# Layer norm, routing and shared branch merged into one block, with the router's logits between the transposes, in a two-layer cross-attention and mixture-of-experts kernel

## The reference

```python
x = x + tanh(g_ffn[0]) * ffn0(layernorm(x))
...
x = x + tanh(g_ffn[1]) * ffn1(layernorm(x))

def ffn0(x, w1s, w2s, w3s, W1, W2, W3, Wg):        # 8 experts, width 1024, one per token
    shared = gelu(x @ w1s) * (x @ w2s) @ w3s
    idx = argmax(x @ Wg)
    return shared + geglu of expert idx
def ffn1(x, W_gate_router, expert_bias, Wg, Wu, Wd, Wg_s, Wu_s, Wd_s):   # 8 experts, width 192, two per token
    scores = sigmoid(x @ W_gate_router)
    sel = top_2(scores + expert_bias)
    w = scores[sel] / sum(scores[sel])
    return silu(x @ Wg_s) * (x @ Wu_s) @ Wd_s + sum_k w[k] * expert_sel[k](x)
```

## Time and profile before

| | us |
|---|---|
| median of 3 timed runs (1776.4 to 1784.43) | 1779.78 |
| the profiled execution's own time | 1767.28 |
| its span | 1765.5 |
| PE busy | 1484.7 (84%) |
| DVE busy | 1160.5 (66%) |
| ACT busy | 856.5 (49%) |
| POOL busy | 237.3 (13%) |

### The profile page before, as it was taken

The page is one execution under the profiler, slowest core; times in us unless marked ns, Lnnn a source line. Parts: engine busy times, 40 slices in busy tenths (PEclk is TensorE's granted clock), DMA queues, the critical chain, the costliest instruction groups (busy, mean ns, idle before and its releaser), DMA issues. The chain is left out here.

```text
span 1765.5 us, 23798 instructions
## 1 busy us (share of the span) xinstructions
PE 1484.7 (84%) x7833; PEld 870.6 (49%) x7834; DVE 1160.5 (66%) x2277; ACT 856.5 (49%) x1537; POOL 237.3 (13%) x357
## 2 busy tenths in 40 slices
PE   5769889779996999994499999999999999675883
PEld 3333333367885788883253333433443434553551
DVE  5739889464112677775399999999999973531334
ACT  3214777522212555551317777777777786231110
POOL 2000000001202333331000000000000000064443
PEclk9787999878998999997659999999999999697997
DMA  8844121120103899982533211111121100525114
GB/s 287 349 143 136 44 56 46 42 92 13 38 1 129 292 341 341 332 314 81 153 87 89 46 25 42 30 24 24 32 40 24 24 2 1 119 78 164 39 42 164
DMA packets 107534, 190.84 MB, mean 108 GB/s; under 512 B 10702, under 2 KB 80323, under 8 KB 107431
## 3 DMA queue, kind: packets, MB, share of 16 engines
q1 hardware_dynamic: 97521, 159.31, 28.7%
q0 software_dynamic: 7584, 27.93, 4.3%
q10 hardware_dynamic: 2326, 2.31, 0.4%
HBM read 145.20 MB, written 43.79 MB: 107 GB/s over the span
## 5 line engine op out<-in xcount | busy, mean ns | idle before, releaser
L1099 DVE TENSOR_REDUCE attend_piece_max<-attend_p_bank 128x1 f32<-128x400 f32 (+3 forms) x1280 | 669.5, 589 | 66.5 <-PE attend_p_bank L982 54.3
L1079 ACT ACTIVATE attend_probs<-attend_s_bank 128x512 f32<-128x512 f32 (+1 forms) x1053 | 549.6, 606 | 232.4 <-PE attend_s_bank L996 232.1
L982 PE MATMUL attend_p_bank<-attend_k_st,attend_q_st 62*128 62x400 f32 (+2 forms) x1280 | 416.0, 435 | 41.6 <-DMA attend_q_st<-q_rows 19.4
L996 PE MATMUL attend_s_bank<-attend_q_st,attend_k_st 64*128 64x512 f32 (+1 forms) x1053 | 390.3, 447 | 39.4 <-ACT attend_probs L1079 13.2
L996 PEld LDWEIGHTS attend_s_bank<-attend_q_st,attend_k_st 64*128 64x128 f32 (+1 forms) x1053 | 168.3, 184 | 347.3 <-ACT attend_probs L1079 326.0
L1013 PE MATMUL attend_o_bank<-attend_probs,attend_v_st 128*32 128x512 f32 (+1 forms) x2176 | 291.0, 607 | 2.2 <-ACT attend_probs L1079 2.1
L982 PEld LDWEIGHTS attend_p_bank<-attend_k_st,attend_q_st 62*128 62x128 f32 x1280 | 208.6, 195 | 89.4 <-issue 39.1
L1753 DVE TENSOR_TENSOR slots_w_low<-slots_w_up,slots_w_high 128x2048 fp32r<-128x2048 f32 x46 | 110.4, 2402 | 45.7 <-ACT slots_w_high L1749 45.7
L1540 DVE TENSOR_TENSOR share_hid<-share_b_bank,share_g_act 128x512 f32<-128x512 f32 (+1 forms) x40 | 27.6, 691 | 116.5 <-PE share_b_bank L1389 105.4
L957 POOL COPY attend_v_st<-attend_values 128x64 f32<-128x64 f32 (+1 forms) x32 | 9.2, 296 | 692.2 <-PE attend_o_bank L1013 658.3
L1749 ACT ACTIVATE slots_w_high<-slots_w_up 128x2048 fp32r<-128x2048 f32 x46 | 87.7, 1908 | 5.9 <-DMA slots_w_up<-in_L_ffn_W_dram 5.7
(11 more groups left out here) (264 smaller groups left out, 1844.2 us busy)
## 6 DMA issues: line engine op xcount, KB each, us to landing
slots_w_up<-in_L_ffn_W_dram SPq DMA_DIRECT2D x46, 1024.0 KB, 7.2
slots_w_dn<-in_L_ffn_W_dram SPq DMA_DIRECT2D x23, 1024.0 KB, 5.6
prep_raw<-in_mask_BxSxS_ik_dram POOLq DMA_DIRECT2D x16, 800.5 KB, 8.4
attend_q_st<-q_rows SPq DMA_DIRECT2D x64, 128.0 KB, 3.1
sorted<-keep_zeros SPq DMA_DIRECT2D x6, 1088.0 KB, 7.8
k_rows<-prep_k_part SPq DMA_DIRECT2D x8, 800.5 KB, 6.0
attend_k_st<-k_rows SPq DMA_DIRECT2D x32, 200.1 KB, 3.6
collect_back<-back SPq DMA_DIRECT2D x12, 512.0 KB, 7.0
```

Source lines behind the costliest of these rows:

```text
L982: last = pe.matmul(bank[:, 0:even(kn)], q_st[rows, slot, t * P:(t + 1) * P].bitcast(F32R), k_st[rows, slot, k0:k0 + even(kn)].bitcast(F32R ...
L996: last = pe.matmul(out, k_st[rows, hs, kt * P:kt * P + kn].bitcast(F32R), q_st[rows, hs, q0:q0 + CH].bitcast(F32R), start=True, stop=not m ...
L1079: act.activation(probs[0:kn, (kt + hs) % RING, q0:q0 + CH], score_bank(i, h, hs, kt, c)[0:kn, :], ACT.Exp).then_inc(exp_done, 1)
L1099: dve.tensor_reduce(dst, bank_of(i, n)[:, 0:kn], AX.X, ALU.max).then_inc(entry_done, 1)
```

## The change

`normalise` is no longer called for the feed-forward parts: its steps stand inside `route_and_share`, in the banks of the shared branch, with ACT alone copying out. On PE the logits of two tiles follow each turn from the third on. In layer 1 the ranking, the placing and then the weights of the two choices (`weigh`) come ahead of the shared branch's first product. Waits on the weights become narrower. In layer 0's slots the first slot's weights are loaded, rounded and split in quarters. The additions of the shared result become 16 of one tile, one behind each of 16 scatters, in both layers. Layer 1's slots load the first slot's rows by themselves, and `collect` cuts its first four tiles into one and three.

```diff
-            pe.wait_ge(router_in, 16 * (l + 1))
-            for t in range(QT):
-                for b in range(DB):
-                    last = pe.matmul(r_bank[:, t], x_nt[:, b, t * P:(t + 1) * P], w_rt[:, b], start=(b == 0),
-                                     stop=(b == DB - 1))
-            last.then_inc(logits_ready, 1)
-            pe.wait_ge(w_in, 48)
...
+            def turn(n):
+                if n >= 4:
+                    pe.wait_ge(copied, n - 3)
...
+                last.then_inc(turned, 1)
+
+            def logits(n):
+                pe.wait_ge(copied, n + 1)
...
+            turn(0)
+            turn(1)
+            pe.wait_ge(router_in, 16)
+            for n in range(2, QT // 2):
+                turn(n)
+                logits(n - 2)
+            logits(QT // 2 - 2)
+            logits(QT // 2 - 1).then_inc(logits_ready, 1)
+            if l == 1:
+                rank()
+            pe.wait_ge(copied, QT // 2)
...
+                        if n == 0:
+                            pe.wait_ge(w_split, which + 1)
...
-                if c == 0:
+                if c == 0 and l == 0:
                     rank()
...
-            round_x(0)
-            act.wait_ge(w_in, 48)
...
+            act.wait_ge(stable, 1)
+            act.activation(std[:, :], var[:, :], ACT.Sqrt).then_inc(rooted, 1)
+            for n in range(QT // 2):
+                copy_out(n)
+            if l == 1:
+                score()
+            act.wait_ge(w_in, 32)
+            act.wait_ge(copied, QT // 2)
             for which in range(2):
                 act.activation(w_high[:, which].bitcast(F32R), w_up[:, which], ACT.Copy).then_inc(w_rounded, 1)
-            round_x(1)
-            act.wait_ge(logits_ready, 1)
-            act.activation(scores[:, :, :], r_bank[:, :, :], ACT.Copy if l == 0 else ACT.Sigmoid).then_inc(logits_act, 1)
+                round_x(which)
+            if l == 0:
+                score()
...
-            for c in range(2):
-                split_x(c)
...
+            if l == 0:
+                for n in range(2):
+                    split_w(n)
+                    split_x(n)
...
+                for n in range(2):
+                    split_w(n)
+                    split_x(n)
+
+            def weigh():
                 for k in range(K):
...
+            if l == 1:
+                place_tokens()
+                weigh()
...
-                if c == 0:
+                if c == 0 and l == 0:
                     place_tokens()
...
+            def load_first():
+
+                e = expert_of(0)
+                for half in range(HV):
+                    for n in range(2):
+                        sp.dma_start(loaded(0, half)[:, n], io[m.pre + m.up[n][1]][e].rearrange("a (b p) f -> p (a b) f", p=P)
+                                     [:, :, half * HW:(half + 1) * HW]).then_inc(quarter_in[2 * half + n], 16)
...
+                if isinstance(s, int) and s == 2:
+                    for n in range(4):
+                        sp.wait_ge(quarter_low[n], 1)
+                elif not first(s, 2):
+                    wait(sp, w_split, s * HV - 2 * HV, apart=True)
+                if first(s):
+                    load_first()
+                else:
+                    load_up(s, slot)
...
-            for t in range(0, QT, 4):
-                pool.tensor_tensor(x_now[:, t:t + 4], x_now[:, t:t + 4], acc[:, t:t + 4], ALU.add).then_inc(summed, 1)
             for s in range(NS):
...
                     .then_inc(y_stored[s % 2], 16)
+                if s < QT:
+                    pool.tensor_tensor(x_now[:, s], x_now[:, s], acc[:, s], ALU.add).then_inc(summed, 1)
...
-                    if not first(s):
+                    if first(s):
+                        pe.wait_ge(quarter_low[2 * half + which], 1)
...
             for half in range(HV):
-                round_weights(act, 0, 0, half)
+                for n in range(2):
+                    act.wait_ge(quarter_in[2 * half + n], 16)
+                    act.activation(w_high[:, half, n].bitcast(F32R), loaded(0, half)[:, n], ACT.Copy)\
+                        .then_inc(quarter_high[2 * half + n], 1)
...
-            sp.dma_start(rows[:, 0:HEAD], tiles[:, 0:HEAD]).then_inc(head_in, 16)
+            sp.dma_start(rows[:, 0:1], tiles[:, 0:1]).then_inc(first_in, 16)
+            sp.dma_start(rows[:, 1:HEAD], tiles[:, 1:HEAD]).then_inc(head_in, 16)
...
+            pool.wait_ge(first_in, 16)
+            stage_rows(0)
             pool.wait_ge(head_in, 16)
-            for s in range(HEAD - 1):
+            for s in range(1, HEAD - 1):
...
-                if s >= NS - QT // 4:
-                    t = 4 * (s - NS + QT // 4)
-                    pool.tensor_tensor(x_now[:, t:t + 4], x_now[:, t:t + 4], acc[:, t:t + 4], ALU.add).then_inc(summed, 1)
+                t = s - HEAD - 1
+                if t < QT:
+                    pool.tensor_tensor(x_now[:, t], x_now[:, t], acc[:, t], ALU.add).then_inc(summed, 1)
...
-        landed = [sc.sem(f"landed{n}") for n in range(4)]
+        cuts = [0, 1, 4, 8, 12, QT]
+        landed = [sc.sem(f"landed{n}") for n in range(len(cuts) - 1)]
...
-                        dve.wait_ge(landed[t // 4], 16)
+                        if t in cuts:
+                            dve.wait_ge(landed[cuts.index(t)], 16)
                         add(t, 0, final)
...
-                    normalise(nc, const, f"norm_f{l}", x_now, stats, x_nt, x_n)
-                    route_and_share(nc, io, const, scratch, m, x_nt, x_n, acc, place, weight, slot_expert, resident)
+                    route_and_share(nc, io, const, scratch, m, x_now, stats, x_nt, x_n, acc, place, weight, slot_expert, resident)
```

More of the change, by code:

```diff
@@ L1345, in _ @@
                     pool.tensor_copy(x_n[:, :, D], const["index"][:, 0:QT]).then_inc(numbered, 1)
+                pool.wait_ge(scaled, QT)
                 pool.wait_ge(placed, k + 1)
@@ L1455, in first_best, with split_w @@
                 then(dve.tensor_tensor(picked[:, k], eno, best[:, 1].unsqueeze(2).to_broadcast(wide), ALU.is_equal))
-            for which in range(2):
+            def split_w(which):
                 dve.wait_ge(w_rounded, which + 1)
@@ L1598, in has_next, with loaded @@
             return not (isinstance(s, int) and s >= NS - 1)
+        def loaded(slot, half):
+            return w_up[:, slot, :, :, half * HW:(half + 1) * HW]
         @block.sync
@@ L1622, in body @@
                 load_rows(s, slot)
-                if not first(s, 2):
-                    wait(sp, w_split, s * HV - HV, apart=True)
-                load_up(s, slot)
+                if isinstance(s, int) and s == 2:
[7 more added lines that the diff above has]
+                    load_up(s, slot)
                 if not first(s, 3):
@@ L1679, in go_up @@
             def go_up(s, slot, half):
-                wait(pe, w_split, s * HV + (half + 1))
+                if not first(s):
+                    wait(pe, w_split, (s - 1) * HV + (half + 1))
                 products = [(x, w, b) for b in range(DB)
```

75 lines of the change are left out of this document (57 added, 18 removed).

## The result

| first timing, 8 runs of each kernel | us |
|---|---|
| kernel before, median (1776.4 to 1785.84) | 1782.28 |
| changed kernel, median (1768.82 to 1781.07) | 1774.18 |
| ratio, with its 95% interval | 0.9951 (0.9936 to 0.9967) |
| changed kernel's profiled execution: own time, span | 1775.59, 1773.8 |

The change gained about 8 us where 21.8 were forecast.

The account below looks back on a forecast made before the run. PE waiting on layer 0's routing chain, and layer 1's scatters, were taken as the bounds. Terms 6.0 + 7.2 + 6.8 + 1.3 + 0.5 = 21.8 us, off the median 1779.78, gave 1758; range 1745 to 1769.

Parts of the forecast that it names:

- Merged block, layer 0, 6.0 us: Layer 0's routing stretch: PE starts the shared branch at 397.4 instead of 403.44, a gain of 6.0 us.
- Merged block, layer 1, 7.2 us: Layer 1's routing: earlier logits and placing bring the first scatter at 1547.8, a gain of 7.2 us.
- the rival of the rising clock: PE's clock rises above 1.2 GHz in mixed transposes and logits; gain over 28 us, at most 39; chance 0.15.
- one row at 0.50: Layer 0's clock window at 389, during the logits: read as PE busy yet throttled, hence turns costed at 1.2 GHz.
- Layer 0's slots, 6.8 us: Start of layer 0's slots: quarters and POOL's additions leaving start the second slot at 572.6 against 579.49, 6.8 us.
- The lower bound of 3.4: Start of layer 0's slots: if the quarters were worth nothing, POOL's additions leaving would still gain 3.4 us.
- Layer 1's slots, 1.3 us, and the collection, 0.5: Layer 1's slots start 1.3 us sooner with one tile of rows first; layer 0's finer collection cut gains 0.5 us.
- the steps don't depend on what makes the difference: Carry-over to timed runs: their median is 12.5 us above the profiled execution, yet the full 21.8 us gain applies.
- That cover is thin but holds, and an overrun of 3 us would cost less than 1: Layer 1's shared branch ends at 1588 to 1591, last scatter issued 1590.6; 3 us overrun costs under 1.
- The rival: Part of the gain is hidden or taken back, 3 us to layer 1's shared branch; gain 9 to 15 us, chance 0.17.

Follow-up runs that it names:

- halt_before: The kernel before with 62 idle copies (19.2 us) on DVE ahead of the second product of layer 1's second chunk; 1769.8 us, ratio 1.0016.
- old_order: Changed kernel, but layer 1 keeps the old order inside the merged block (weights and first chunk on DVE before the placing); 1747.7 us, ratio 0.989.

## Why the prediction was wrong

Most of the mechanisms hold, and the sum comes out where nothing disturbs them. Taken from the profiled execution the forecast was 1745.5; the changed kernel's medians in the three later timings are 1744.1, 1747.3 and 1746.6, 21 to 25 us under the kernel before. That the sum fits is partly luck: the block brought 17.2 us instead of 13.2, the slots and the collection 5.3 instead of 8.6. Term by term:

- *Merged block, layer 0, 6.0 us.* 27.0 became 21.3 us, **5.7**, at 1.2 GHz throughout as costed. The 27.0 are one execution's: with the old block the stretch takes 27.0 to 27.3 us in three traces (mean granted clock 0.71 over its first 16 us) and 28.5 to 28.9 in four (0.61), so that up to 7.6 us are gained.
- *Merged block, layer 1, 7.2 us.* 42.7 to 35.0 is **7.7** at 1.2 GHz and up to **13.9** where the clock rose. What the rival of the rising clock describes thus happens half of the time, in layer 1; its gain of over 28 us was in no timing. I gave 0.15 to it on the strength of one row at 0.50, and a single execution can't carry that. I also misread the rows there: PE wasn't busy all the time but for 1.11 of the 2.5 us at 379, and it stood idle for 2.76 us ahead of the logits. The Trainium skill ("TensorE: Matmul & The Clock Gate", Part 1) has activity release the throttle. The traces agree only in part: PE was busy for all of the windows at 1504 and 1506 above, and the granted clock was 1.00 in one and 0.50 in the other.
- *Layer 0's slots, 6.8 us.* **5.7** to the second slot, some 6 to the last product. The lower bound of 3.4 stood for the additions' leaving alone; with the quarters in place it brings 0.8, and alone it wasn't measured. The Trainium skill ("Advanced Engine Details and Errata", VectorE Performance Modes) says that GpSimd instructions and VectorE instructions that use two ports block each other. That the split takes 3.06 us beside the additions and 2.29 without agrees with this, though no row tells whether the subtraction uses two ports.
- *Layer 1's slots, 1.3 us, and the collection, 0.5.* **0**, nothing that the traces tell from their scatter. Layer 0's collection takes 14.6 to 15.8 us from its first load with the new cut and 14.8 to 15.1 with the old one.

The steps that failed are two. The first is the one that carried the sum over to the timed runs: *"the steps don't depend on what makes the difference"* between the profiled 1767.28 and the median 1779.78. In the one trace from that timing, of the changed kernel, they do. It has 28 us of halts: 6 in layer 0 (155.6 us from the shared branch's start to the slots, against 149.3 to 150.3 in every other execution) and 22 in layer 1 (98.1 us from the first transpose to the slots' rows, against 76.1 in the two executions whose first scatter came equally soon). The second is *"That cover is thin but holds, and an overrun of 3 us would cost less than 1"*. In quiet runs it holds, by 3.6 to 4.9 us. The rival priced its loss at 3 us, and it is 15 with one stop of 19 us. The kernel before hides nearly all of such a stop, as `halt_before` shows. It was the order in layer 1 that spent the cover, for 1.0 us; `old_order` kept the 6.6 us that the merge brings there (42.7 to 36.1) and a lead of 20.2. That it would hide a stop as the kernel before does is argued from this lead, as no run put a stop into it.

What is shown is that a stop of this size in this place takes the gain back from the changed kernel and hardly touches the kernel before. What is only argued is that the first timing's runs all had such halts, as there is one trace of them. Open stays where the halts come from: none of 18 later traces of either kernel or a variant has one, and they didn't return. They stand in the same stretches in which records of updates are missing, so that the recording itself is a rival that nothing here rules out. Open, too, is what made the kernel before 14 us slower there. No trace of it from one of those eight runs exists; by the covers found here, the halts of 6 and 22 us would have cost it 6 in layer 0 and 3 in layer 1, an estimate of 9 us that leaves 5 unexplained.

## What to carry to other kernels

When the profiled execution lies 0.5% under the fastest timed run, ask what the timed runs have that the trace lacks, before adding a sum to their median. A reordering that shortens the chain by using up the cover of a second chain should be priced with the cover that is left (here 19 us became 4, for 1 us), since this decides what a disturbance costs. And a delay put in by hand must stand where its engine isn't idle already.

## What the runs showed of the hardware

- In one trace PE's semaphore updates are recorded up to 15 us behind the ends of the products that they announce (0.01 to 0.02 us in the others), and ACT and DVE start only then, while POOL goes on: it issued a scatter every 1.26 to 1.45 us through the halt at 1557.8 to 1564.1. All of this lies between the first scatter of a layer and the few microseconds behind the last, as do the gaps in the records. Waiting for instructions isn't seen: no packet of the two instruction queues lies between 431.8 and 467.1 or between 1528.3 and 1585.5. The Trainium skill ("NOTIFIC — The notification-queue block", 7.1) describes settings in which a full queue of records drops the new one, and one in which it stalls the engine that produces them. The 568 missing records agree with dropping; no run here shows whether anything stalled.
- PE's granted clock in the same instruction sequence, PE fully busy, was 0.50 in one execution and 1.00 in the next; in layer 1 that alone is worth 3 to 6 us.
